# Local attention: the queries' norms taken into the exponential's scale and the maximum, instead of into the queries

## What is computed

```python
def l2norm(t):
    return t / jnp.clip(jnp.linalg.norm(t, axis=-1, keepdims=True), 1e-12)

def _layer(x, wqkv, qs, ksc, wo, ...):
    qkv = shift_token(x) @ wqkv
    q, k, v = jnp.split(qkv, 3, axis=-1)          # to heads
    q = l2norm(q) * qs
    k = l2norm(k) * ksc
    q, k = rotary_xpos(q, k)
    o = local_attention(q, k, v)                  # sim = (8 q) k^T, masked to the window and the one before
    x = x + o @ wo                                # attn = softmax(sim); o = attn v
    ...
```

## Time and profile before

| | us |
|---|---|
| median of 3 runs (3964.82 to 3969.65) | 3964.98 |
| the profiled execution | 3962.53 |
| its span, first to last instruction | 3960.7 |
| PE busy | 3417.7 (86%) |
| DVE busy | 2567.4 (65%) |
| ACT busy | 1771.5 (45%) |
| POOL busy | 990.3 (25%) |
| mean granted TensorE clock | 0.978 |

### The profile page before, as it was taken

One profiled execution on the slowest core, in us unless ns is written; L12 is line 12 of the kernel. 1 busy time (PEld: TensorE's weight loads), 2 busy tenths in 40 slices (PEclk: granted clock), 3 DMA queues, 4 the chain that ended last, 5 costly groups with the idle time before them and its releaser, 6 DMA issues. The chain is left out here.

```text
span 3960.7 us, 55447 instructions
## 1 busy us (share of the span) xinstructions
PE 3417.7 (86%) x19803; PEld 1783.7 (45%) x19959; DVE 2567.4 (65%) x5513; ACT 1771.5 (45%) x3776; POOL 990.3 (25%) x855
## 2 busy tenths in 40 slices
PE   5888898888988889888988889888898889888877
PEld 2345434444344443444344443444434444444444
DVE  5666765666567665666656665666656666576675
ACT  1454444543444535544344444445354453444424
POOL 3032311332023310333113330233203331133224
PEclk8999999999999999999999999999999999999988
DMA  4100101102011021000110020110200001100130
GB/s 163 33 12 28 39 31 33 36 4 68 2 33 38 1 69 32 12 28 34 36 33 31 8 65 4 33 38 1 69 27 18 28 30 40 33 27 13 61 89 22
DMA packets 82300, 138.66 MB, mean 35 GB/s; under 512 B 10566, under 2 KB 56808, under 8 KB 79588
## 3 DMA queue, kind: packets, MB, share of 16 engines
q1 hardware_dynamic: 75972, 120.91, 9.6%
q10 hardware_dynamic: 3744, 6.61, 0.6%
q0 software_dynamic: 2304, 7.46, 0.5%
HBM read 105.06 MB, written 29.10 MB: 34 GB/s over the span
## 5 line engine op out<-in xcount | busy, mean ns | idle before, releaser
L652 DVE TENSOR_REDUCE nmax<-banks 128x1 f32<-128x512 f32 (+3 forms) x1216 | 760.1, 658 | 391.9 <-PE banks L462 205.2
L572 ACT ACTIVATE probs<-banks 128x512 f32<-128x512 f32 (+3 forms) x1024 | 475.5, 527 | 292.7 <-PE banks L481 204.6
L462 PE MATMUL banks<-ks,qs 72*128 72x512 bf16 (+3 forms) x1536 | 440.8, 332 | 86.4 <-DVE nmax L652 61.0
L481 PE MATMUL banks<-qs,ks 74*128 74x512 bf16 (+3 forms) x1536 | 446.9, 331 | 46.8 <-ACT probs L572 17.2
L113 PE MATMUL banks<-filler,identb 128*128 128x512 bf16 x1632 | 415.9, 383 | 14.8 <-PEq L445 7.6
L462 PEld LDWEIGHTS banks<-ks,qs 72*128 72x128 bf16 x1536 | 140.9, 98 | 371.5 <-DVE nmax L652 214.6
L572 ACT ACTIVATE early<-banks 128x256 f32<-128x256 f32 (+3 forms) x512 | 194.3, 442 | 168.1 <-PE banks L481 166.7
L1518 ACT ACTIVATE probs<-banks,nm 128x192 f32<-128x192 f32 x512 | 172.1, 421 | 206.7 <-DVE nm L1470 206.7
L113 PEld LDWEIGHTS banks<-filler,identb 128*128 128x128 bf16 x1776 | 170.2, 98 | 203.5 <-issue 57.2
L531 PE MATMUL banks<-probs,v 128*32 128x512 f32 (+3 forms) x2048 | 236.2, 533 | 19.1 <-DVE att L639 10.3
L1552 POOL TENSOR_TENSOR probs<-probs,inv 128x768 f32<-128x768 f32 x128 | 187.0, 1466 | 253.6 <-DVE inv L1480 253.6
(11 more groups left out here) (523 smaller groups left out, 6659.3 us busy)
## 6 DMA issues: line engine op xcount, KB each, us to landing
qs<-parts_scratch SPq DMA_DIRECT2D x300, 96.0 KB
ks<-parts_scratch SPq DMA_DIRECT2D x288, 96.0 KB
parts_scratch<-parts SPq DMA_DIRECT2D x50, 384.0 KB, 2.5
shared<-in_w_h SPq DMA_DIRECT2D x17, 1024.0 KB, 7.9
shared<-in_w SPq DMA_DIRECT2D x26, 256.0 KB, 3.9
qs<-max_parts SPq DMA_DIRECT2D x192, 4.0 KB
xn<-in_x SPq DMA_DIRECT2D x9, 256.0 KB, 2.8
factor_scratch<-g SPq DMA_DIRECT2D x8, 256.0 KB, 2.3
```

Source lines behind the costliest of these rows:

```text
L462: mm = nc.tensor.matmul(K.ps[:, b, i * keys:(i + 1) * keys], K.qs[0:72, 4 * g + j, t * P:(t + 1) * P], K.ks[0:72, 4 * g + j, 0:keys], star ...
L481: mm = nc.tensor.matmul(K.ps[:, b, q0:T], K.ks[0:KR, h, k * P:(k + 1) * P], K.qs[0:KR, h, q0:T], start=True, stop=not on_tensor)
L572: nc.scalar.activation(probs[:, 4 * (q % QUADS) + m % 4, q0:T], K.ps[:, bank("second", m), q0:T], ACT.Exp, scale=scale).then_inc(exped, 1)
L652: nc.vector.tensor_reduce(nmax[:, t, h:h + len(heads)], K.ps[:, n % 2, 0:len(heads) * keys].rearrange("p (j k) -> p j k", k=keys), AX.X, A ...
```

## The change

The queries are no longer multiplied by their norms. `rn` of both blocks is kept in one tile `K.rn` of 128 x 4 x 2 x 8, and a local attention multiplies each unit's four negated maxima by the four factors (a new DVE `tensor_tensor` of 128 x 4, behind a new wait on the maxima, `peaked`) and gives each exponential the factor of its rows as `scale`, a column of 128 x 1 read from SBUF. PE's transposes of queries wait for the rotation's sum (`added`) instead of `q_scaled`. `neghalf` becomes smaller, and waits that only guarded `q_scaled` or the reuse of the old `rn` fall away. The keys are scaled as before.

```diff
@@ local_qkv
-            if t:
-                dve.wait_ge(rn_ready, t)
-                dve.wait_ge(added, 2 * t - 1)
-                scale_heads(nc.vector, t - 1, 0).then_inc(q_scaled, 1)
...
         def turn(t):
             for m in range(2):
-                pe.wait_ge((q_scaled, k_scaled)[m], t + 1)
+                if m == 0:
+                    pe.wait_ge(added, 2 * t + 1)
+                else:
+                    pe.wait_ge(k_scaled, t + 1)
...
-            pool.wait_ge(rn_ready, t + 1)
             if t < NT - 1:
+                pool.wait_ge(rn_ready, t + 1)
                 pool.wait_ge(added, 2 * t + 2)
-                scale_heads(nc.gpsimd, t, 1).then_inc(k_scaled, 1)
-            else:
-                pool.wait_ge(added, 2 * t + 1)
-                pool.wait_ge(q_scaled, NT - 1)
-                scale_heads(nc.gpsimd, t, 0).then_inc(q_scaled, 1)
+                scale_keys(nc.gpsimd, t).then_inc(k_scaled, 1)
@@ local_attention, vector
                     nc.vector.tensor_reduce(nm[:, u, :, :], s[:, :, :, 64:256], AX.X, ALU.max,
-                                            negate=True).then_inc(lowered, 1)
+                                            negate=True).then_inc(peaked, 1)
+                    p = w // 2
+                    norms = K.rn[:, 2 * u:2 * u + 2, 0, 2 * p:2 * p + 2].rearrange("p i e -> p e i")
+                    dve.wait_ge(peaked, w + 1)
+                    nc.vector.tensor_tensor(nm[:, u, :, :], nm[:, u, :, :], norms, ALU.mult).then_inc(lowered, 1)
@@ local_attention, scalar
                             a = nc.scalar.activation(probs[:, w % RING, e, i, 64:256],
                                                      K.ps[:, 2 * u + e, 256 * i + 64:256 * i + 256], ACT.Exp,
+                                                     scale=K.rn[:, 2 * u + i, 0, 2 * p + e:2 * p + e + 1],
                                                      bias=nm[:, u, e, i:i + 1])
@@ GluThenQkv, tensor
                 if m == 0:
-                    pe.wait_ge(self.q_scaled, t + 1)
+                    pe.wait_ge(self.added, t + 1)
@@ GluThenQkv, vector, step 6 of a tile
-                dve.wait_ge(self.added, t + 1)
-                scale(0).then_inc(self.q_scaled, 1)
```

More of the change, by code:

```diff
@@ L1227, in local_qkv @@
 def local_qkv(nc, K, ctx, shifted):
-    (projected, squared, v_copied, summed, clipped, rn_ready, rotated, q_scaled, k_scaled,
-     qk_turned, copied, vec, added, k_added) = K.pool[0:14]
+    (projected, squared, v_copied, summed, clipped, rn_ready, rotated, k_scaled,
+     qk_turned, copied, vec, added, k_added) = K.pool[0:13]
     w = K.w2_qkv[0]
@@ L1237, in local_qkv, with scale_keys @@
     ssq = sbuf(nc, ctx, "ssq", [P, NT, 2, LH])
-    rn = sbuf(nc, ctx, "rn", [P, NT, 2, LH])
-    def scale_heads(engine, t, m):
-        x3 = qk[:, t % 2, m, :].rearrange("p (h d) -> p h d", d=LD)
-        return engine.tensor_tensor(x3, x3, rn[:, t, m, :].unsqueeze(2).to_broadcast([P, LH, LD]), ALU.mult)
+    rn = K.rn
+    def scale_keys(engine, t):
+        x3 = qk[:, t % 2, 1, :].rearrange("p (h d) -> p h d", d=LD)
+        return engine.tensor_tensor(x3, x3, rn[:, t, 1, :].unsqueeze(2).to_broadcast([P, LH, LD]), ALU.mult)
     def tensor(pe, banks_free):
@@ L1343, in vector @@
         dve.wait_ge(k_scaled, NT - 1)
-        scale_heads(nc.vector, t, 1).then_inc(k_scaled, 1)
+        scale_keys(nc.vector, t).then_inc(k_scaled, 1)
     def gpsimd(pool):
@@ L1367, in local_attention @@
     (scored, lowered, exped, zeroed, summed, inverted, scaled, turned, copied, kept, weighed, oT_ready,
-     projected) = K.pool[0:13]
+     projected, peaked) = K.pool[0:14]
     RING, UNITS, SPAN = 3, LH, P + WIN
@@ L1511, in exps @@
                 def exps(w):
-                    u = w % 2
+                    p, u = divmod(w, 2)
                     act.wait_ge(lowered, w + 1)
@@ L1697, in __init__ @@
         (self.turned2, self.shifted2, self.qk_done, self.v_done, self.squared, self.summed, self.rn_done, self.rotated,
-         self.added, self.q_scaled, self.k_scaled, self.qk_turned, self.copied, self.v_copied, self.vec2,
-         self.clipped) = K.pool[38:54]
+         self.added, self.k_scaled, self.qk_turned, self.copied, self.v_copied, self.vec2,
+         self.clipped) = K.pool[38:53]
         self.k_added, self.late_added, self.late_scaled = K.pool[54:57]
@@ L1704, in __init__ @@
         self.ssq = sbuf(nc, ctx, "ssq2", [P, 2, 2, LH])
-        self.rn = sbuf(nc, ctx, "rn2", [P, 2, 2, LH])
         self.shift2 = copy_shifted(nc, K, self.turned2, self.shifted2, 7)
@@ L1791, in vector @@
                 if t >= 2:
-                    dve.wait_ge(self.q_scaled, t - 1)
-                    if t - 2 < self.LATE:
-                        dve.wait_ge(self.k_scaled, t - 1)
+                    dve.wait_ge(self.rn_done, t - 1)
                 for m in range(2):
@@ L1807, in vector @@
             elif i == 6:
-                dve.wait_ge(self.rn_done, t + 1)
-                scale = lambda m: nc.vector.tensor_tensor(
-                    heads(self.qk[t % 2][m]), heads(self.qk[t % 2][m]),
-                    self.rn[:, t % 2, m, :].unsqueeze(2).to_broadcast([P, LH, LD]), ALU.mult)
                 if t >= self.LATE:
+                    x = heads(self.qk[t % 2][1])
+                    dve.wait_ge(self.rn_done, t + 1)
                     dve.wait_ge(self.late_added, t - self.LATE + 1)
-                    scale(1).then_inc(self.late_scaled, 1)
-                dve.wait_ge(self.added, t + 1)
-                scale(0).then_inc(self.q_scaled, 1)
+                    nc.vector.tensor_tensor(x, x, K.rn[:, t, 1, :].unsqueeze(2).to_broadcast([P, LH, LD]),
+                                            ALU.mult).then_inc(self.late_scaled, 1)
             else:
@@ L1845, in gpsimd @@
                 pool.wait_ge(self.clipped, t + 1)
-                if t >= 2:
-                    pool.wait_ge(self.q_scaled, t - 1)
-                nc.gpsimd.tensor_tensor(self.rn[:, t % 2, :, :].rearrange("p m h -> p (m h)"),
+                nc.gpsimd.tensor_tensor(K.rn[:, t, :, :].rearrange("p m h -> p (m h)"),
                                         self.ssq[:, t % 2, :, :].rearrange("p m h -> p (m h)"), K.neghalf[:, 0:2 * LH],
@@ L1860, in gpsimd @@
                 x = self.qk[t % 2][1].rearrange("p (h d) -> p h d", d=LD)
-                nc.gpsimd.tensor_tensor(x, x, self.rn[:, t % 2, 1, :].unsqueeze(2).to_broadcast([P, LH, LD]),
+                nc.gpsimd.tensor_tensor(x, x, K.rn[:, t, 1, :].unsqueeze(2).to_broadcast([P, LH, LD]),
                                         ALU.mult).then_inc(self.k_scaled, 1)
@@ L2388, in build_kernel @@
         K.ident = sb("ident", [P, P])
-        K.neghalf = sb("neghalf", [P, 2 * NT * LH])
+        K.neghalf = sb("neghalf", [P, 2 * LH])
         K.stats = sb("stats", [P, NT, 6])
@@ L2393, in build_kernel @@
         K.rstd = sb("rstd", [P, 2 * NT])
+        K.rn = sb("rn", [P, NT, 2, LH])
         K.up_late, K.down_late = sb("up_late", [P, E3 - NOW, 4 * P]), sb("down_late", [P, E3 - NOW, 2, D])
```

## The result

| | before | after |
|---|---|---|
| median of 4 runs each, us | 3966.82 (3964.82 to 3969.65) | 4083.54 (4078.58 to 4090.64) |
| ratio, 95% interval | | 1.030 [1.029, 1.031] |
| span of the profiled execution | 3960.7 | 4076.7 |
| PE busy / ACT busy | 3417.7 / 1771.5 | 3486.8 / 1817.8 |
| mean granted TensorE clock | 0.978 | 0.960 |

The changed kernel is slower by 117 us, 3.0%. The forecast of 4047 had the direction, and the measured time lies just above its range of 4005 to 4082.

What follows compares the result with a forecast made beforehand. PE was busiest overall, but the local attentions were taken as bound by a closed ring of DVE and ACT. The terms 118 - 27 - 9 = 82 us on the median 3964.98 gave 4047, range 4005 to 4082.

Steps and rivals of the forecast that it cites:

- The hold of the product by POOL: Local attention: the new DVE product is held until POOL's SBUF-reading product ends, so the exponentials start 0.72 us later.
- ring: Local attention: one unit's closed cycle of DVE and ACT, from its sums to the next sums, 3.43 us before.
- The exponentials' longer pitch: Local attention: the scale operand adds 90 ns to each exponential's pitch, so a group of four grows by 0.36 us.
- Ring 4.51, an attention 7.4 us longer, 118 in all: Local attentions: a unit takes 3.43 + 0.72 + 0.36 = 4.51 us; with the first units, 16 x 7.4 = 118 us added.
- local_qkv 27 less: Local projections: the fourth projection, third transposes and last transposes lose 1.41, 1.71 and 0.29 us of delay; 8 x 3.4 = 27.
- the sum: Whole kernel: 118 - 27 - 9 = 82 us added to the median of 3964.98, giving 4047.
- The long attention 9 less: Long attention: of 32 dropped DVE products only PE's waits for them count, 9.1 us in all, so 9 us less.
- Behind the last sums nothing changes: End of each local attention: no time is added or lost after the last sums, 0 us.
- The clock rival: Local attentions: PE's clock falls to 0.50, some units exceed the ring, 16 x 1.5 = 24 us more: 4071; chance 12%.
- a clock in the local attentions that isn't 1.00: Local attentions: a sign in the changed kernel's profile that would show the prediction wrong.
- Nothing for the stages that the change does not touch: Unedited stages of each batch, some 273 us: the prediction gave them no term, 0 us.

Runs made afterwards that it cites:

- the gains alone: The changed kernel with the local attention of before, without new product and scale operand, queries' norms left out: 3951.4 us against 3963.2 for the kernel before, ratio 0.998.
- the fillers in the ring: The changed kernel with filler matmuls in PE's idle time in local-attention units 2, 4 and 6: 4061.3 us against 3964.9 for the kernel before, ratio 1.024.
- the costs alone: The kernel before with the changed local attention reading ones as norms, queries still multiplied in the projections: 4131.5 us against 3962.9 for the kernel before, ratio 1.043.

## Why the prediction was right or wrong

- *The hold of the product by POOL* (0.72 us a ring): right, 0.68 to 0.69 against 0.16; with one input in PSUM it is gone.
- *The exponentials' longer pitch* (0.36 a group): right, 1.72 instead of 1.36; alone it makes the ring 3.80.
- *Ring 4.51, an attention 7.4 us longer, 118 in all*: 4.51 to 4.52, 7.40, 118.4.
- *local_qkv 27 less*: 32. The wait of the fourth projection went from 1.70 to 0.23, the other two are gone, as worked out. The fourth projection starts 1.47 us earlier behind the stage's start (1.41 in the sum), the third transposes 3.34 (3.12) and the last ones 3.85 (3.41), and the first maxima come 4.01 earlier. So the path was right and the term 5 us too small; why the two last waits were worth 0.16 and 0.21 us more than the idle time ahead of them is open.
- *The long attention 9 less*: 8.5 in this execution, and that is luck. A long attention without a fall of the clock takes 95.4 us before and 93.85 after, and one with the fall some 42 us in takes some 1.9 more, in both kernels. So the change is worth 1.56 us a batch, 12.5 in all where the sum had 9, and two more falls (seven instead of five) took 4 of them. With the gains alone, where only two attentions have the fall, it was 18.
- *Behind the last sums nothing changes*: the first step that failed. PE's idle time in the longer ring, which the sum took as harmless, lets the clock fall, and the tail, where PE is last, pays: 18.5 us, shown by the fillers in the ring, which took them away.
- *The clock rival*: its mechanism was right and its place half right. It asked for two slow units on end before the maxima are late. The changed kernel's profile has none, and the price came behind the ring; in the kernel with the costs alone it happened in four rings, for 0.8 to 0.9 us each. Its 24 us for the attentions is near the 18.5 by luck, since it was priced in the ring and paid in the tails. It was given 12%, but its sign, a clock in the local attentions that isn't 1.00, came true: 11 of the 16 rings have a fall in their middle. The row for it was misread in part: in the earlier trace rows the microsecond with 0.65 us of work is itself at 0.50, and only the one with 0.40 stands ahead of the fall.
- *Nothing for the stages that the change does not touch*: the second step that failed, 20.8 us. Over all the runs such a rest takes from 272.8 to 286 us with the same instructions, and the runs with a delay show that which it is depends on where it stands in time. The kernel before stood well: 272.8 to 272.9 in four of seven rests. The changed kernel and the five with parts of the change all have a higher mean than its 273.6, from 274.1 to 279.2. What sets the place from one execution to the next was not tried; in the three traces with fillers in these stages the falls move on when one place is filled, so that the price of each single fall is read from the rows (1.7 us at 634), not shown by taking it away.

With both, and with 5 us more for `local_qkv`, the sum would have been 82 + 19 + 21 - 5 = 117 us: 4082. Of these the 21 could not have been worked out ahead: the next kernel or execution has another number there.

## What to carry to other kernels

When a change lengthens a stage in which TensorE is not last, count TensorE's idle time there and price the clock's fall in the stage behind, where it is last; a few fillers in the idle places are the test, and here the remedy. In a kernel of hundreds of microseconds of unchanged stages, allow for a shift in time alone: here from -0.4 to +1.2% for a pure delay; and to tell a gain of that size from luck, add a pure delay to both kernels and look again. Where a small VectorE product must stand beside a GpSimd product, let one of its inputs come from PSUM: here that took the product from 0.68 to 0.16 us.

## What was not expected of the hardware

The same idle stretch of TensorE brings a fall of the granted clock in one pass and none in the next: 0.35 and 0.00 us of work in two microseconds, then 1.00 in one kernel and 0.50 in the other. The time of one unchanged stretch takes some values again and again, in kernels that differ elsewhere (272.8, 274.5, 275.1, 276.7, 278.6, 280.2). The Trainium skill (TensorE: Matmul & The Clock Gate, Part 1) states that the chip's watch over the activity runs on freely and does not start anew with the kernel. The runs fit that, since a pure delay of 0.85 us a batch made one kernel 14.6 us faster and one of 1.1 us made another 48 us slower; the watch itself is in no row.

Such a kernel's own time spreads too: with the gains alone ten runs lie between 3940 and 3973 us, while with four fillers more four runs lie between 3935.5 and 3937.4.
